# A pair's last spread on GpSimd: the relative queries first, then the high and low ones

## What is computed

```python
scores = jnp.einsum('bhld,bhrd->bhlr', Q, K) * scale
scores = scores + jnp.einsum('bhld,lrd->bhlr', Q, rel_k)
attn = jax.nn.softmax(scores, axis=-1)
out = jnp.einsum('bhlr,bhrd->bhld', attn, V)
out = out + jnp.einsum('bhlr,lrd->bhld', attn, rel_v)
...
x = x + attention(layernorm(x));  x = x + experts(layernorm(x))
```

## Time and profile before

| | |
|---|---|
| median of 3 runs | 2175.84 us (2170.8 to 2176.1) |
| profiled execution | 2177.57 us |
| its span, first to last instruction | 2175.8 us |
| mean granted TensorE clock | 0.987 of full speed |
| busy share of the span | PE 96%, DVE 75%, ACT 70%, POOL 53% |

### The profile page before, as it was taken

How to read it: one execution, slowest core, us unless ns; L and a number is a source line. 1 busy time by engine, 2 the same in 40 slices (tenths; PEclk the granted TensorE clock), 3 DMA queues, 4 the chain that set the end, 5 groups by cost and what they waited for, 6 DMA issues and landing times.

```text
span 2175.8 us, 88171 instructions
## 1 busy us (share of the span) xinstructions
PE 2093.9 (96%) x37442; PEld 1547.5 (71%) x37442; DVE 1638.7 (75%) x3856; ACT 1514.6 (70%) x3304; POOL 1161.7 (53%) x1104
## 2 busy tenths in 40 slices
PE   2999999999999999999999999999998999999998
PEld 1777777677777767776777777677775777777776
DVE  4787787788778877977887787788875667667675
ACT  3666676666666666776666676666665888888886
POOL 5554446356345644454554445444424777677776
PEclk8999999999999999999999999999998999999999
DMA  5112211321221122113212211222112112212210
GB/s 138 33 54 66 73 54 44 82 63 48 67 81 44 54 66 72 54 46 83 64 54 65 73 54 44 65 71 56 54 44 32 28 21 24 29 19 24 29 20 11
DMA packets 255682, 114.49 MB, mean 53 GB/s; under 512 B 142218, under 2 KB 251156, under 8 KB 255348
## 3 DMA queue, kind: packets, MB, share of 16 engines
q1 hardware_dynamic: 255348, 109.60, 20.5%
HBM read 83.34 MB, written 8.39 MB: 42 GB/s over the span
## 4 chain that ended last, share of the span: by engine, by line
PE 83%; POOL 5%; ACT 5%; issue 3%; SPq 1%; DVE 1%; DMA 1%; ACTq 0%; POOLq 0%; DVEq 0%
PE ps L1270 20%; PE ps L1205 11%; PE ps L1290 10%; PE ps L1212 8%; PE ps L1300 8%; PE ps L1223 7%; POOL probs_t L539 3%; ACT probs L686 2%; PE ps L1435 2%; PE ps L1452 2%; PE ps L1437 2%; PE ps L1436 2%; PE ps L1454 2%; PE ps L1453 2%; PE ps L1308 1%
## 5 line engine op out<-in xcount | busy, mean ns | idle before, releaser
L618 ACT ACTIVATE probs<-ps,neg_max 128x512 f32<-128x512 f32 x1024 | 690.6, 686 | 357.9 <-DVE neg_max L813 357.9
L813 DVE TENSOR_REDUCE neg_max<-ps 128x1 f32<-128x512 f32 x1024 | 636.1, 683 | 175.3 <-PE ps L1212 170.7
L463 POOL TENSOR_TENSOR stat_hi<-q_twice,mask8h 128x1024 f16<-128x1024 f16 x128 | 242.8, 1897 | 689.4 <-PE ps L1212 623.7
L1270 PE MATMUL ps<-const,probs 128*128 128x128 f32 x4096 | 498.0, 274 | 17.1 <-issue 16.3
L1270 PEld LDWEIGHTS ps<-const,probs 128*128 128x128 f32 x4096 | 453.6, 141 | 46.6 <-issue 33.6
L818 DVE COPY probs_t<-ps 128x512 f32<-128x512 f32 x512 | 339.8, 684 | 93.2 <-PE ps L1270 90.6
L539 POOL TENSOR_TENSOR probs_t<-probs,probs_t 128x1024 f16<-128x1024 f32 x160 | 340.2, 2135 | 111.0 <-ACT probs_t L692 111.0
L608 ACT ACTIVATE probs_t<-ps 128x512 f32<-128x512 f32 x512 | 279.0, 595 | 133.3 <-PE ps L1270 130.6
L1205 PE MATMUL ps<-keys,stat_hi 128*32 128x512 f16 x4096 | 321.6, 387 | 0.0
L1212 PE MATMUL ps<-rk_split,stat_rel 96*32 96x512 f16 (+2 forms) x4096 | 283.9, 342 | 0.0
L1019 DVE SCALAR_TENSOR_TENSOR keys<-ps,comb,keys 128x128 f32<-128x128 f32 x640 | 179.7, 343 | 129.6 <-PE ps L1454 129.6
(11 more groups left out here) (135 smaller groups left out, 2907.7 us busy)
## 6 DMA issues: line engine op xcount, KB each, us to landing
rv_step<-in_rv_win SPq DMA_DIRECT2D x128, 512.0 KB, 3.9
keys<-keys SPq DMA_DIRECT2D x64, 96.0 KB, 2.7
x_pair<-in_x SPq DMA_DIRECT2D x8, 512.0 KB, 4.4
q_twice<-q_hi SPq DMA_DIRECT2D x32, 128.0 KB, 2.8
q_lo_pair<-q_lo SPq DMA_DIRECT2D x32, 128.0 KB, 2.5
rel_scratch<-rel_t SPq DMA_DIRECT2D x256, 16.0 KB, 3.2
x_pair<-in_x SPq DMA_DIRECT2D x16, 256.0 KB, 3.1
x_pair<-rel_scratch SPq DMA_DIRECT2D x64, 64.0 KB, 3.9
```

What stands on the lines that cost most here:

```text
L618: nc.scalar.activation(probs[:, q, :], ps[:, i, :], ACT.Exp, bias=neg_max[:, q:q + 1], accum_out=row_sum[parity][:, s * QUADS + q:s * QUAD ...
L813: nc.vector.tensor_reduce(neg_max[:, q:q + 1], ps[:, i, :], op=ALU.max, axis=AX_X, negate=True).then_inc(max_done, 1)
L1270: last = nc.tensor.transpose(ps[:, bank, rt * P:(rt + 1) * P], probs[:, q, rt * P:(rt + 1) * P], ident)
```

## The change

In step 15 of each pair POOL writes `stat_rel` first, then `stat_hi` and `stat_lo`. ACT's wait ahead of `q_rel` goes from "all four counts of step 15" to "the first count of step 15". SP's wait ahead of the copies into `q_twice` goes from "all but the last count" to "all four".

```diff
 def copy_queries(pair, first):
     if not first:
-        sp.wait_ge(stat_ready, START + pair * STEPS * STAT_OPS - 1)
+        sp.wait_ge(stat_ready, START + pair * STEPS * STAT_OPS)
...
-                    spread_high(s)
-                    spread_low(s)
-                    if s == 0:
-                        pool.wait_ge(q_rel_ready, START + pair * 4 + 4)
-                    spread_relative(s)
+                    if s == STEPS - 1:
+                        spread_relative(s)
+                        spread_high(s)
+                        spread_low(s)
+                    else:
+                        spread_high(s)
+                        spread_low(s)
+                        if s == 0:
+                            pool.wait_ge(q_rel_ready, START + pair * 4 + 4)
+                        spread_relative(s)
...
 def relative_queries(pair, b, half, bank, first):
     if not first:
-        act.wait_ge(stat_ready, START + pair * STEPS * STAT_OPS)
+        act.wait_ge(stat_ready, START + (pair * STEPS - 1) * STAT_OPS + 1)
```

## The result

The changed kernel takes 2148.78 us (2145.34 to 2150.59, four runs) against 2173.91 us for the kernel before (2170.80 to 2176.10, four runs): ratio 0.9885, 95% interval 0.9873 to 0.9897. That is 25.1 us less; 26.1 us had been forecast, to 2150 us. The two profiled executions are 2177.57 and 2150.59 us, 27.0 apart.

What follows compares the result with a forecast made beforehand. PE was taken to bound the kernel, standing at seven pair boundaries for ACT's copy behind POOL's relative spread. 18.6 us of wait and 7.5 of clock, 26.1 together, lead from a median of 2175.84 to 2150 us, range 2145 to 2159.

Steps and rivals of the forecast that it cites:

- What bounds: PE, busy 96% of the span, stands seven times at pair boundaries, 16.3 us, for ACT's copy, which waits for POOL's relative spread.
- The term of the wait: PE's rounds (13,1) at the seven boundaries lose their wait for ACT's copy into `q_rel`: together 18.6 us less.
- the two boundaries counted with 2.75: Two of seven boundaries where round (13,1) was to give back 2.75 us; the other five 2.6 us.
- The term of the clock: In round (14,0) behind five of seven boundaries the clock stays up when the wait is gone: together 7.5 us.
- 1% is about what these five stretches make: Granted clock 0.99 over 60 to 1600 us, 1% of 1540 us, taken as about the five low-clock stretches behind boundaries.
- Rival 1: At the boundaries the wait goes but the clock still falls: only 18.6 us come back, 2157 us; chance 0.13.
- The sum: Wait and clock at the boundaries together: 18.6 + 7.5 = 26.1 us less, giving 2150 us.
- POOL's 0.48 us: At the last boundary the relative spread would end at 1405.98, 0.48 us before ACT is free at 1406.46.
- rival 2: At the boundaries a second wait takes part of the place, as with a longer relative spread: 2153 to 2167 us; chance 0.08.
- The cover of SP's wait: SP comes to the copies into `q_twice` 4.6 us after their later release, so the longer wait costs nothing.
- The slack behind SP: From the next pair's relative spread to PE's need at the last transpose of (15,1): some 4.5 us, unchanged.
- rival 4: SP's copies start the next pair late and the kernel is slower, about 2185 us at 14 us late; chance 0.02.

Runs made afterwards that it cites:

- The two partly late releases: Changed kernel with the relative spread second and ACT waiting for the second count, 2156.65 us; or behind the low spreads and for the third, 2154.30 us.

## Why the prediction was right

**What bounds.** PE's seven waits went with ACT's wait, and the time went with them: right.

**The term of the wait, 18.6 us.** Each (13,1) round lasts 6.58 or 6.59 us after. The seven together are 18.5 us shorter. Right to 0.1 us, though at the two boundaries counted with 2.75 the clock had fallen just before PE went on, so that some 0.15 us at each is the clock's. The two partly late releases lie on the same line: 8.2 us by their rounds where 8 were expected, 5.3 where 4 to 5 were (the medians give 7.9 and 5.5, the ratios 6.5 and 3.3; both traces also have a fall of the clock in the last pair).

**The term of the clock, 7.5 us.** Right: no fall at any boundary after, and 7.2 us when the clock was kept up alone. One support of it does not hold. The 0.99 over 1540 us is rounded and can't carry "1% is about what these five stretches make": 1% would be 15 us, twice the 7.5 that the rounds give. Rival 1 is ruled out here, and with it the reading of the Trainium skill that it leaned on (TensorE: Matmul & The Clock Gate, Why this matters for your kernels), which warns only of longer gaps: stands of 2.4 us did make the clock fall. Each of the three traces with the full stand has falls behind five of the seven, and not the same five, so the 7.5 us are what five falls cost.

**The sum.** Attention gave 26.3 us against 26.1. The medians differ by 25.1. The one of before came out at 2173.91 where the forecast had started from 2175.84, and that the time still landed 1.2 us from 2150 is partly luck of this kind: the medians move by 1 or 2 us from one set of runs to the next.

**Margins.** POOL's 0.48 us ahead of the end of ACT's exponentials was exact; the copy starts 0.12 us before that end, so it ended 1.16 us after the start of PE's transposes (1385.06 against 1383.90) where 1.29 had been worked out. The new neighbours on DVE did not change the spread's 1.96 us; rival 2 did not happen. The cover of SP's wait was named rightly (4.6 us; SP came 4.6 us after POOL's last spread ended, 1391.57 against about 1386.95). The slack behind SP was put at 4.5 us and is some 7 at the last boundary, since POOL's wait for `q_rel` is part of it. When the copies were held for longer (rival 4), the delay had its effect by a second path, the window of relative values, which the prediction named as queued behind the wait but did not price.

## What to carry to other kernels

A count that several results share releases its waiter with the last of them. Where one of them is waited for elsewhere, produce it first and wait for that count alone. The order without the lower count gave nothing (2174.03 us); the lower count without the order would release ACT at the high spread, while POOL has still to read `q_rel`. Before taking a wait to another place, read when its engine gets there: SP came 4.6 us after the release, so the added wait was free, and each thing queued behind it needs its own price. And idle time of TensorE is priced with the clock behind it: here 2.6 us lost in the round itself cost 3.7 on average.

## What the runs showed of the hardware

- Behind stands of 2.41 us the clock fell to 1.2 GHz at some boundaries and not at others: five of seven in the kernel before, and again five of seven in each of the two runs that keep the full stand (the order alone, SP's wait alone). Behind the stands of 2.79 to 4.05 us for the late window it fell at all seven. Stands of about 0.98 us (seven) and 0.56 us (seven) had none behind them. A fall behind a stand of 2.41 us made round (14,0) 1.25 to 1.68 us longer.
- Repeated 128 x 128 transposes of f32 kept the clock up as real work does: seven stands filled with 2.35 us of them, no fall.
- A 512 KB window issued behind five other loads took 4.9 to 7.0 us from the start of its issue to landing, in eleven traces in which nothing around it had been changed, and PE waited 0.3 to 3.0 us for it; with four of the loads issued elsewhere it took 3.9 us and PE did not wait.
